# A two-layer convolution block: three offset phases in a row, a third row buffer, additions between two selections, norms in two halves

## The reference, cut to what matters

```
x = x + L0(gn(x))      # depthwise 3x3, then three 32x32 channel mixes
x = x + L1(gn(x))      # deformable 3x3 convolution:
  off    = conv3x3(gn(x), w_off)                 # 64 channels: a row and a column offset per pixel
  rows, cols = clip(off + own position)
  v_lt, v_rb, v_lb, v_rt = x at floor/ceil(rows), floor/ceil(cols)
  mapped = bilinear mix of the four
  out    = conv3x3(mapped, w_conv) + b_conv
```

## Time and profile before

| what | value |
|---|---|
| median of 3 runs | 778.83 us (774.56 to 778.92) |
| the profiled execution's own time | 773.91 us |
| its span, first to last instruction | 772.1 us |
| mean granted TensorE clock | 0.951 |
| busy: PE / DVE / ACT / POOL | 657.6 / 517.1 / 445.2 / 496.9 us |

### The profile page before, as it was taken

How to read it: one execution, slowest core, us unless ns; L and a number is a source line. 1 busy time by engine, 2 the same in 40 slices (tenths; PEclk the granted TensorE clock), 3 DMA queues, 4 the chain that set the end, 5 groups by cost and what they waited for, 6 DMA issues and landing times. The chain is left out here.

```text
span 772.1 us, 16851 instructions
## 1 busy us (share of the span) xinstructions
PE 657.6 (85%) x6572; PEld 226.6 (29%) x6572; DVE 517.1 (67%) x959; ACT 445.2 (58%) x774; POOL 496.9 (64%) x413
## 2 busy tenths in 40 slices
PE   4798866878979988999979988989879989687876
PEld 4332222223323332323323332323223333222222
DVE  3685877347873688468874688467785695668552
ACT  7245656466655754576656754576646755576630
POOL 4022846388666875869566875859558876979550
PEclk9999989879999999999999999999999999998978
DMA  8949420479647794589547894589547504465546
GB/s 144 189 100 173 70 56 2 116 163 170 114 109 185 155 176 110 127 195 185 117 109 183 161 170 110 129 191 184 107 111 180 125 1 100 108 140 137 125 108 146
DMA packets 135798, 101.92 MB, mean 132 GB/s; under 512 B 13825, under 2 KB 112673, under 8 KB 135713
## 3 DMA queue, kind: packets, MB, share of 16 engines
q1 hardware_dynamic: 111680, 89.01, 54.7%
q10 hardware_dynamic: 24032, 11.78, 8.1%
HBM read 31.59 MB, written 16.78 MB: 63 GB/s over the span
## 5 line engine op out<-in xcount | busy, mean ns | idle before, releaser
L775 PE MATMUL off_ps<-x1a,wo 32*64 32x512 f32 x4608 | 285.6, 620 | 32.8 <-ACT col_mask_ps L978 24.4
L665 PE MATMUL c_ps<-mapb,w 128*64 128x512 f32 x336 | 166.1, 635 | 39.7 <-DVE x1a L1397 38.9
L665 PE MATMUL c_ps<-xb,w 128*64 128x512 f32 x336 | 153.0, 602 | 8.8 <-ACT x1a L926 8.8
L775 PEld LDWEIGHTS off_ps<-x1a,wo 32*64 32x64 f32 x4608 | 94.0, 135 | 203.1 <-issue 132.7
L667 PE MATMUL c_ps<-xa,w 128*64 128x512 f32 x336 | 153.0, 602 | 0.0
L1412 DVE COPY_PREDICATED other_row<-row_mask_ps,row_diff 128x768 f32<-128x768 int32 x128 | 123.8, 1020 | 34.9 <-ACT row_mask_ps L971 29.6
L667 PE MATMUL c_ps<-mapa,w 128*64 128x512 f32 x294 | 146.8, 640 | 0.0
L1208 POOL TENSOR_TENSOR other_row<-other_row,x_strips 128x512 f32<-128x512 f32 x48 | 57.2, 1193 | 129.2 <-DVE other_row L1424 129.2
L952 ACT ACTIVATE other_row<-row_diff 128x768 f32<-128x768 f32 x128 | 101.1, 841 | 50.8 <-POOL mapped L1222 27.8
L1369 DVE BATCH_NORM_STATS2 stats<-x1a 128x6 f32<-128x512 f32 x64 | 42.8, 686 | 118.0 <-ACT x1a L926 118.0
L1209 POOL TENSOR_TENSOR other_col<-other_col,other_row 128x512 f32<-128x512 f32 x64 | 89.0, 1391 | 50.4 <-DVE other_row L1424 50.4
(11 more groups left out here) (127 smaller groups left out, 822.1 us busy)
## 6 DMA issues: line engine op xcount, KB each, us to landing
mapa<-mapped SPq DMA_DIRECT2D x224, 65.0 KB, 2.1
mapb<-mapa SPq DMA_DIRECT2D x28, 520.0 KB, 5.7
out_dram<-x1a SPq DMA_DIRECT2D x49, 256.0 KB, 4.7
xb<-in_x_dram SPq DMA_DIRECT2D x48, 256.0 KB, 8.1
xa<-in_x_dram ACTq DMA_DIRECT2D x40, 256.0 KB, 7.2
x_strips<-x1a SPq DMA_DIRECT2D x112, 81.2 KB, 2.1
x_strips<-x1a SPq DMA_DIRECT2D x112, 65.0 KB, 2.0
xa<-in_x_dram SPq DMA_DIRECT2D x16, 256.0 KB, 7.6
```

Of the source, the lines that this page charges most:

```text
L665: nc.tensor.matmul(bank[0:64, :], weights[:, kx, :], rows_b[:, of, kx:kx + W], start=(kx == 0), stop=(kx == 2))
L775: last = nc.tensor.matmul(off_ps[r % 2][64 * t:64 * t + 64, CH * (r // 2):CH * (r // 2) + CH], wo[wpar][q, 3 * ky + kx, :], x1a[par][q, b: ...
```

## The change

PE runs the three phases of a pair directly one behind the other, and then all groups of the pair. `other_row` gets a third buffer, so ACT copies the rows of both chunks of a pair ahead of the masks; the copy of the left values becomes an operation of its own (`copy_side`). DVE's `deform` is split into `select_rows` and `select_columns`, and the additions of c2 groups stand between them (`in_parts` hands out one group per place); the statistics of x1 come behind both chunks. ACT takes x1 groups out after the even chunk's masks, after the odd chunk's, and between the two `sum_far`. `pad_x1`, `pad_x` and `clamp(i + 1, 0)` move ahead of the masks of a pair. `norm` is cut into means and rates, which may stand at different places (`fill_up`). POOL's row steps move ahead of the waits of chunks 2, 3, 6 and 7. conv2 takes its groups in another order, and in SP's queue the store of the first half moves ahead of the move of mapped. conv2's weights have one buffer (the last image takes w1[0]). In image 0 a third group stands in the first pair and one fewer later.

```
-    FIRST_CONV1 = [[3], [4], [5], [6], [7], [], [], []]
+    FIRST_CONV1 = [[3], [4, 5], [6], [7], [], [], [], []]
...
-    CONV2_GROUPS = [0, 2, 4, 6, 1, 3, 5, 7]
-    STORE_AFTER = [6, 8]
+    CONV2_GROUPS = [0, 2, 1, 3, 4, 6, 5, 7]
+    STORE_AFTER = [4, 8]
...
+    X_STATS, X_STATS_0 = [5, 5, 6, 7], [1, 1, 3, 3]
+    PAD_X_0 = 2
+    STEPS_0, STEPS_1 = [6, 7], [2, 3]
...
+            jobs += [("b1", i + 1, 0)] if i >= 2 and k == 0 else []
...
-        if 0 < i < NB - 2 and k == FURTHER_BIAS[i]:
-            jobs += [("b1", i + 2, 0)]
...
-        behind, n = [[], [], []], 1
-        for job in jobs_behind(i, 2 * u) + jobs_behind(i, 2 * u + 1):
-            behind[n].append(job)
-            if job[0] in ("x1", "c2"):
-                n = min(n + 1, 2)
-        return behind
+        return jobs_behind(i, 2 * u) + jobs_behind(i, 2 * u + 1)
+    def in_parts(jobs, n):
+        parts = [[]]
+        for job in jobs:
+            if parts[-1] and parts[-1][-1][0] in ("x1", "c2") and len(parts) < n:
+                parts.append([])
+            parts[-1].append(job)
+        return parts + [[]] * (n - len(parts))
...
-        other_row = [sb(f"other_row{n}", [P, 3, KR, WQ]) for n in range(2)]
+        other_row = [sb(f"other_row{n}", [P, 3, KR, WQ]) for n in range(3)]
...
-        w2 = [sb(f"w2{n}", [P, 3, 2 * C]) for n in range(2)]
+        w2 = [sb("w2", [P, 3, 2 * C]), w1[0]]
...
-                if prev:
-                    sp.wait_ge(mapped_ready, NK * i + 4)
-                    sp.wait_ge(conv2_done, 8 * (i - 1) + 4)
-                    sp.wait_ge(mapped_pads, 2 * i + 1)
-                    move_mapa(0)
                 if prev and after:
                     sp.wait_ge(out_ready, 8 * (i - 1) + STORE_AFTER[0])
                     store(sp, i - 1, (i - 1) % 3, 0)
+                if prev:
+                    sp.wait_ge(mapped_ready, NK * i + 4)
+                    sp.wait_ge(conv2_done, 8 * (i - 1) + 6)
+                    sp.wait_ge(mapped_pads, 2 * i + 1)
+                    move_mapa(0)
...
-                    for ky, jobs in enumerate(pair_jobs(i, u)):
+                    for ky in range(PHASES):
                         if NP * i + u >= 1 or ky >= 1:
                             pe.wait_ge(off_phases, PHASES * (NP * i + u) + ky)
                         offsets_phase(i % 2, i % 3, u, ky)
-                        for job in jobs:
-                            job_of(job)
+                    for job in pair_jobs(i, u):
+                        job_of(job)
...
             def copy_rows(i, k):
-                n = k % 2
+                g = NK * i + k
+                if g >= 3:
+                    act.wait_ge(mapped_ready, g - 2)
+                act.wait_ge(diff_ready, 2 * (NK // 2 * i + 2 * (k // 4) + k % 2 + 1))
+                rows = other_row[g % 3]
...
+                last.then_inc(rows_copied, 1)
+            def copy_side(i, k):
                 g = NK * i + k
                 if g >= 2:
                     act.wait_ge(mapped_ready, g - 1)
-                act.wait_ge(diff_ready, 2 * (NK // 2 * i + 2 * (k // 4) + k % 2 + 1))
-                for odd in range(2):
-                    act.activation(other_row[n][:, :, KR // 2 * odd:KR // 2 * odd + KR // 2, :],
-                                   diffs_3(diffs_of(k), 2 * (k // 2 % 2) + odd), ACT.Copy, scale=-1.0)
-                act.activation(split(other_col[n][:, :, :]), of_chunk(i, k, 0), ACT.Copy).then_inc(rows_copied, 1)
+                act.activation(split(other_col[k % 2][:, :, :]), of_chunk(i, k, 0), ACT.Copy).then_inc(side_copied, 1)
...
                     if prev and u == 0:
                         pad_map(i - 1, (i - 1) % 3)
-                    if i == 0 and u == FURTHER_BIAS[0] // 2:
+                    copy_rows(i, e)
+                    copy_side(i, e)
+                    copy_rows(i, o)
+                    if nxt and u and ("x1", i + 1, 7) in pair_jobs(i, u - 1):
+                        pad_x1(i + 1, (i + 1) % 3)
+                    if nxt and u == NP - 1:
+                        clamp(i + 1, 0)
+                    if u == 0 and i >= 2 and nxt:
+                        pad_x(i + 1, (i + 1) % 2)
+                    if i == 0 and u == PAD_X_0:
                         pad_x(i + 2, i % 2)
-                    copy_rows(i, e)
-                    for job in behind[0] + behind[1]:
                     if u == 0:
                         act.wait_ge(bo_ready, i + 1)
                     act.wait_ge(off_phases, PHASES * (NP * i + u + 1))
                     row_mask(i, e)
                     lengths(i, e)
                     col_mask(i, e)
-                    lengths(i, o)
-                    for job in behind[2][:1]:
+                    for job in parts[0]:
                         evacuate(job)
                     row_mask(i, o)
+                    copy_side(i, o)
+                    lengths(i, o)
                     col_mask(i, o)
-                    copy_rows(i, o)
+                    for job in parts[1]:
+                        evacuate(job)
+                    sum_far(i, e)
+                    for job in parts[2]:
+                        evacuate(job)
+                    sum_far(i, o)
                         clamp(i, 1)
                     if u == 2:
                         pad_mapped(i, i % 3, 1)
-                    if nxt and u and ("x1", i + 1, 7) in sum(pair_jobs(i, u - 1), []):
-                        pad_x1(i + 1, (i + 1) % 3)
-                    if after and i and u == NP - 1:
-                        pad_x(i + 2, i % 2)
-                    if nxt and u == NP - 1:
-                        clamp(i + 1, 0)
-                    for job in behind[2][1:]:
+                    for job in parts[3]:
                         evacuate(job)
-                    sum_far(i, e)
-                    sum_far(i, o)
...
+                    row = other_row[(NK * i + k) % 3]
+                    if k in STEPS_1:
+                        row_steps(i, 1, STEPS_1.index(k))
+                    if i + 1 < NB:
+                        for right in range(2):
+                            if k == STEPS_0[right]:
+                                row_steps(i + 1, 0, right)
                     pool.wait_ge(products_ready, NK * i + k + 1)
...
-                    if k in (1, 2):
-                        row_steps(i, 1, k - 1)
-                    elif k >= NK - 2 and i + 1 < NB:
-                        row_steps(i + 1, 0, k - (NK - 2))
...
-            def norm(stats, pair, rstd, mean_ready):
-                half_var = pair[:, 1:2]
+            def means(stats, pair, mean_ready):
...
+            def rates(pair, rstd):
+                half_var = pair[:, 1:2]
...
             def prepare_conv2(i, wpar, par):
-                served = max(i - 1, 0) if isinstance(i, int) else i
-                if not (isinstance(i, int) and served == 0):
-                    dve.wait_ge(conv2_done, 8 * served)
+                if wpar:
+                    dve.wait_ge(conv1_done, 8 * NB - 8)
+                elif not (isinstance(i, int) and i == 0):
+                    dve.wait_ge(conv2_done, 8 * i)
...
-            def deform(i, k):
-                n = k % 2
+            def select_rows(i, k):
...
                 dve.wait_ge(rows_copied, g + 1)
                 dve.wait_ge(row_mask_ready, g + 1)
...
                 last.then_inc(row_selected, 1)
+            def select_columns(i, k):
...
+                dve.wait_ge(side_copied, g + 1)
                 dve.wait_ge(col_mask_ready, g + 1)
                 step(dve.copy_predicated(split(side), split(cols), of_chunk(i, k, 2)))
                 dve.wait_ge(row_selected, g + 1)
...
+            def fill_up(i, u, place):
+                prev, nxt, after = i >= 1, i + 1 < NB, i + 2 < NB
...
+                if prev and now == 1:
+                    prepare_conv2(i - 1, 0, (i - 1) % 3)
+                if prev and now == 3:
+                    dve.wait_ge(beyond_ready, NK * i)
+                    step(dve.reduce_max(far_image[:, i - 1:i], far[(i - 1) % 2][:, :], AX))
+                if not nxt and now == END_BIAS:
+                    prepare_conv2(i, 1, i % 3)
+                if nxt and place == 1 and ("x1", i + 1, 7) in pair_jobs(i, u):
+                    x1_means(i + 1, (i + 1) % 3)
+                    x1_norm(i + 1, (i + 1) % 2, (i + 1) % 3)
+                if after:
+                    at = X_STATS if i else X_STATS_0
+                    for half in range(2):
+                        if now == at[half]:
+                            x_stats(i + 2, half)
+                    if now == at[2]:
+                        x_means(i + 2, i % 2)
+                    if now == at[3]:
+                        x_norm(i + 2, i % 2)
             for i in range(NB):
-                prev, nxt, after = i >= 1, i + 1 < NB, i + 2 < NB
                 for u in range(NP):
-                    behind = pair_jobs(i, u)
```

(44 more changed lines are left out.)

52 lines of the change are left out of this document (33 added, 19 removed).

## The result

The changed kernel takes **723.73 us** (median of 4 runs, 721.68 to 727.02) against 778.38 for the kernel before: ratio 0.9313, 95% interval 0.9273 to 0.9353. The forecast was 714, range 700 to 760. The profiled execution took 722.83 us, its span is 721.0, and 708.0 had been worked out for that span: 13.0 too little.

A forecast was written before the change was run, and what follows sets the result against it. PE's gaps of 2 to 7 us and the half clock behind them bound it; 772.1 less 2 (image 0), 22 (1), 32.6 (2 to 5), 2.1 (6), 6.1 (7), plus 0.7, gives span 708.0, median 714; range 700 to 760.

The forecast's parts named there:

- the forecast case: Whole kernel: the change works as worked out, 714 us, own range 700 to 726; chance 0.54.
- the signs that it names as wrong: ACT idle for a strip before pair 3's row mask, POOL releasing ACT while PE idles, late additions, images above 82 us.
- SP's queue: SP's DMAs per image: 85 at 0.65 make 55 of 79 us; earlier stores end ACT's 28.3 us of waits.
- PE's own work: PE in middle images: three phases 8.71 us a pair, a group 2.65; image taken as 79.2, ends 77.9 and 82.1.
- ACT frees off_ps in time: Behind the third phase: masks need 6.4 us, four groups cover 10.6; 24.4 us of waits remain only in images 0, 7.
- Additions between selections: DVE's c2 additions reach PE's banks with 0.7 to 1.7 us spare; 38.9 us of waits go except the tail's 7.41.
- Third buffer, nothing: ACT's copies of both chunks' rows wait only for the chunk three before; no cost expected.
- what is put ahead of the masks: Clamp and border fill precede pair 3's masks: strips there at 58 us, masks at 67; 9 spare and 4.2 cover.
- the slower rival: Strips' first half over 13.2 us late stops PE in images 1 to 6; at 26, 77 more, 791; chance 0.06.
- Image 1, 22 us gained: Image 1: earlier border fill and strips, 72.5 us, 22 less; 11 if only the clock came back.
- Image 0, 2 us gained: Image 0, bound by DVE: both norms in pair 1 bring ACT's fill about 1 us sooner; 2 us taken, 0 to 8.
- POOL late: Rival: POOL's row steps slow beside DVE, 2.9 us late twice per image; at half, 17 more, 731; chance 0.13.

The follow-up runs named there:

- SP's order repaired: Changed kernel; from image 2 SP loads xb's second half behind the strips' first half; in image 1 all xb precedes strips, mapped's moves precede the store: 713.57 us, ratio 0.9203.

## Why the prediction was right, point by point

The 723.73 lies in the range, and by 2 us in the 700 to 726 of the forecast case itself. The gains that it names for masks, additions and image 1 came about, near to what was worked out. Yet two of the signs that it names as wrong came too: ACT stood ahead of pair 3's masks for a strip, and images 2 and 5 took over 82 us. The term that failed is SP's queue.

- **PE's own work, 8.71 a pair and 77.9 to 79.2 an image:** right. The phases took 8.77 to 8.78 and image 6 78.0; images 2 to 5, at 80.7 to 82.8, reach this only with SP's order repaired (78.2 to 79.2).
- **ACT frees off_ps in time, the 24.4 us remain in images 0 and 7:** right, 15.6 there, and 1.16 behind two groups, where 1.1 had been worked out. But with ACT's and DVE's order moved along, the masks did not need the phases together where a pair has three groups behind them. What did was the bias job at the image's start, which the prediction did not cost.
- **Additions between selections, 38.9 us gone:** right in the waits, 9.2. But of the 29.7 us that went, 19.1 go without the new places too (19.8 are left with additions in twos). What the places earn in time: nothing that the noise lets one see in the changed kernel (723.73 for 725.93), and 7 us with the stores' order undone, 5.4 of it in image 1.
- **The norm's means between the chunks:** credited with part of that; worth nothing (712.30 for 713.57).
- **Third buffer, nothing:** it adds no cost, but the rest stands on it. Without it the new order takes 813, more than before. "If POOL were late, the copies of the odd chunk would hold the masks behind them" was the right sentence: with two buffers ACT waits for POOL 56 times.
- **SP's queue, "85 by 0.65, make 55 us of 79":** the term that failed. It is 78.0 of 81.9: eight loads took 15.7 for 5.2, stores 0.75 to 2.0 each, moves 0.7 to 0.85. The trace before already had more than one price: in its turn from 353.17 DMAs held the queue for 69.3 us, with 10.51 for the eight loads and 6.03 for three stores. That sum would still have left some 10 us of room; that the loads would grow by half in the new order no row before showed. With it failed the step on what is put ahead of the masks. The clamp ran 70.6 us into image 3, not at 58, 12.6 late; and the cover was one group, not four, since `bias_o` holds a bank. That is the slower rival's mechanism at a small size: stops of 1.8 to 2.8 us, 9.4 in all, and half clock in images 2 and 5 (PEclk 0.98, 1.7 us each), against the 10.5 that images 2 to 5 are over. No run puts the clamp back behind the masks, so what its place alone costs is not shown. Moving the stores ahead, meant to end 28.3 us of ACT's waits, did so and cost 7.
- **Image 1, 22 us gained:** 19.5. The stop of 1.16 was in the sum (6.4 for two groups). The one of 2.83, behind DVE's norm, where 1.9 was set down, is 0.9 of the 2.5 missing; half clock (PEclk 0.98 of 75.1 us, 1.7 us), of which the sum had none, is about the rest.
- **Image 0, 2 us gained:** it lost 0.7. The bias of image 2's x1 waited 9.97 us for two norms in a row on DVE (before, 5.68 and 2.74 there), and PEclk fell from 0.93 to 0.87 of full speed, 4.6 us more lost to half clock.
- **POOL late:** it did not reach PE. The mean of its products with off_abs grew from 1295 to 1453 ns (L1216, now L1241) while DVE's busy share rose from 67% to 74%, the way the rival had it, under cover; how much of that is due to DVE was not taken apart.

## What to carry to other kernels

Add up each DMA queue over one turn of the loop from rows of its own kinds of transfer, not by one price: a queue that is 95% full makes every reordering on it a change of the pace. An operation moved ahead of others on its engine brings its own wait with it; look how late its releaser is, and which bank or buffer is freed only behind it. Undoing one part of a reordering alone can cost more than the whole gained (80 us for PE's order and 90 for the third buffer, where the whole gained 55), and another part can cost time itself (the stores, 7). So undo parts together with what depends on them, and read in the profile where the time went: several runs here met a forecast's time by another mechanism.

## What the hardware showed that was not expected

What a DMA holds its issuing queue for is no fixed price. The same eight 256 KB loads held SP for 13.9 to 16.8 us in the five turns of the changed kernel, for 10.51 in the kernel before, and in image 3 for 3.90 and 2.26 as two fours with sixteen small moves between them. The traces show one thing that goes with it, the data still under way. In the changed kernel each of the 40 loads of xb from image 1 on was issued with over 1 MB of earlier DMAs not yet landed; an image's first four held SP for 1.36 us each on average, its last four for 2.54. With half of xb later, the first four had as much under way and held it for 1.35; the last four had less than 0.8 MB and held it for 0.58. It is not the whole of it: in the kernel before, all 40 had over 1 MB too and took 1.37. Whether that is the cause was not tried by itself. Taking four stores off SP did not free it by as much either: the sixteen moves beside them grew from 13.50 to 17.20.
